# Setup of a two-layer transformer kernel: first loads in two parts, key splits and gates moved between engines

## What is computed

```python
ga = (2 * (ga >= 0) - 1) * maximum(abs(ga), 0.25)        # gb the same
# layer 0
h = layernorm(x) * (1 + ca) + sa
q, k, v = h @ Wq.T + bq, h @ Wk.T + bk, h @ Wv.T + bv    # 16 heads of 8
x = x + ga * (concat(softmax(q k^T / sqrt(8)) v) @ Wo.T + bo)
h = layernorm(x) * (1 + cb) + sb
x = x + gb * (shared_mlp(h) + top1_of_16_experts(h))
# layer 1: causal attention with 8 query heads over one shared key/value head of 16,
# then a gated feed-forward over each token and the one before it
```

## Time and profile before

| | |
|---|---|
| median of 3 runs | 1148.6 us (1145.84 to 1151.31) |
| profiled execution, its own time | 1150.95 us |
| its span | 1149.2 us |
| PE busy | 1027.6 us (89%) |
| DVE busy | 907.4 us (79%) |
| ACT busy | 819.5 us (71%) |
| POOL busy | 151.0 us (13%) |

### The profile page before, as it was taken

One profiled execution on the slowest core, in us unless ns is written; L12 is line 12 of the kernel. 1 busy time (PEld: TensorE's weight loads), 2 busy tenths in 40 slices (PEclk: granted clock), 3 DMA queues, 4 the chain that ended last, 5 costly groups with the idle time before them and its releaser, 6 DMA issues.

```text
span 1149.2 us, 22211 instructions
## 1 busy us (share of the span) xinstructions
PE 1027.6 (89%) x8772; PEld 351.4 (31%) x8772; DVE 907.4 (79%) x1174; ACT 819.5 (71%) x1581; POOL 151.0 (13%) x270
## 2 busy tenths in 40 slices
PE   4558999999999999999998999899978888798987
PEld 1212222222222222222232444343434453333314
DVE  5797999998999989999988777666766558587603
ACT  3105999998999998999986676467743546466775
POOL 2004100003000013000033000411031003000101
PEclk9757999999999999999999999999989999899987
DMA  4650500002000001000003331142003220200000
GB/s 106 122 103 15 139 2 2 2 2 43 2 2 2 2 15 29 2 1 3 2 1 111 113 100 29 29 89 52 2 1 111 67 63 22 46 10 2 10 2 10
DMA packets 47309, 42.07 MB, mean 37 GB/s; under 512 B 6150, under 2 KB 45414, under 8 KB 47206
## 3 DMA queue, kind: packets, MB, share of 16 engines
q1 hardware_dynamic: 44950, 35.27, 13.1%
q0 software_dynamic: 1824, 5.25, 1.6%
q10 hardware_dynamic: 432, 0.13, 0.0%
HBM read 26.83 MB, written 13.30 MB: 35 GB/s over the span
## 4 chain that ended last, share of the span: by engine, by line
PE 64%; DVE 18%; ACT 7%; DMA 4%; issue 3%; SPq 2%; POOL 1%; DVEq 0%; POOLq 0%; ACTq 0%
PE O L897 23%; PE T L868 12%; DVE mx L1204 10%; PE S L827 7%; PE S L834 4%; ACT PT L1435 3%; PE T L877 3%; PE S L1008 2%; PE S L966 1%; PE S L976 1%; PE T L1016 1%; DMA rows_k<-q 1%; PE S L967 1%; PE S L877 1%; PE T L906 1%
## 5 line engine op out<-in xcount | busy, mean ns | idle before, releaser
L1204 DVE TENSOR_REDUCE mx<-S 128x2 f32<-128x1024 f32 (+2 forms) x672 | 757.6, 1181 | 90.0 <-PE S L834 37.6
L1435 ACT ACTIVATE PT<-T 128x512 f32<-128x512 f32 (+2 forms) x1280 | 675.8, 580 | 118.4 <-PE T L868 47.8
L897 PE MATMUL O<-PT,Va 128*9 128x256 f32 (+1 forms) x4040 | 319.0, 388 | 3.3 <-ACT Os L1470 3.3
L827 PE MATMUL S<-Ks,Qs 48*128 48x512 bf16 x1024 | 208.2, 398 | 27.7 <-DVE mx L1204 20.9
L868 PE MATMUL T<-Qs,Ks 51*128 51x512 bf16 x1024 | 202.3, 388 | 16.0 <-ACT PT L1435 7.2
L868 PEld LDWEIGHTS T<-Qs,Ks 51*128 51x128 bf16 x1024 | 55.6, 93 | 227.1 <-issue 132.4
L897 PEld LDWEIGHTS O<-PT,Va 128*9 128x9 f32 x4040 | 60.0, 88 | 207.7 <-issue 198.3
L834 PE MATMUL S<-K,Qs 96*128 96x512 bf16 (+3 forms) x320 | 85.5, 357 | 15.0 <-DMA Qs<-rows_q 4.7
L877 PE MATMUL T<-Qs,K 99*128 99x512 bf16 (+3 forms) x256 | 72.2, 350 | 7.7 <-ACT PT L1435 4.1
L897 PE MATMUL O<-PT,V 128*17 128x512 f32 (+3 forms) x640 | 76.2, 549 | 0.0
L827 PEld LDWEIGHTS S<-Ks,Qs 48*128 48x128 bf16 x1024 | 52.6, 95 | 54.9 <-DVE mx L1204 47.0
(11 more groups left out here) (276 smaller groups left out, 836.1 us busy)
## 6 DMA issues: line engine op xcount, KB each, us to landing
Qs<-in_L_ffn_experts SPq DMA_DIRECT2D x28, 192.0 KB, 2.9
Ks<-in_L_ffn_experts SPq DMA_DIRECT2D x20, 192.0 KB, 2.6
Qs<-rows_q SPq DMA_DIRECT2D x48, 64.0 KB
Vf<-sorted_x SPq DMA_DIRECT2D x12, 256.0 KB, 4.7
sorted_y<-Vf SPq DMA_DIRECT2D x12, 256.0 KB, 2.3
Qs<-rows_q SPq DMA_DIRECT2D x24, 128.0 KB, 4.4
rows_q<-q SPq DMA_DIRECT2D x7, 384.0 KB, 2.6
sorted_x<-XP POOLq DMA_DIRECT2D x1, 1792.0 KB, 10.8
```

The lines of the kernel that those rows point to most:

```text
L827: m = e.matmul(two[:, i, :], Qs[r0:r0 + 48, hp, q0:q0 + 128], Ks[r0:r0 + 48, hp, CH * kb:CH * kb + CH], start=True, stop=True, tile_positi ...
L897: m = e.matmul(Ob[32 * g:32 * g + d1, lo:hi], v, PT[(2 * j + g // 2) % 4][:, p0 + lo:p0 + hi], start=(kt == 0 and halves[0] == 0), stop=Tr ...
L1204: e.tensor_reduce(mx[:, u % 2, h0:h0 + 2, kb], two[:, :, 0:n], AX.X, ALU.max).then_inc(free, 1)
L1435: e.activation(PT[(2 * j + pair) % 4][:, CH * i + lo:CH * i + CH], bank[:, lo:CH], ACT.Exp).then_inc(free, 1)
```

## The change

Setup order: statistics and norms of chunks 1 and 2 stand before the first splits; key chunks 1 to 3 are split by GpSimd, not VectorE; their projections use banks T2, O and T2. The loads of all four key chunks and of query chunk 0 are made in two parts: pair indices 0 and 1 first, and 2 to 7 in a second `load` that stands, with the late loads, after 16 score tiles. Of the first part of query chunk 0 SyncE issues six DMAs and ScalarE six. The four `values` stand after score tiles 8, 10, 12 and 14 instead of before the first. In the steps, `scaled_weights` moves from 1 to 5, `scaled_weights2` from 3 to 7, the projection of q chunk 1 from 5 to 9, `late_pool` from 8 to 11, `late_constants` from 12 to 14. `broadcast` and the arithmetic of `gates` go from VectorE to GpSimd; ScalarE copies the gates, `bias_v` and `rows` out of PSUM; GpSimd adds `bias_v` to the bias ahead of `scale`.

```diff
--- before.py
+++ after.py
@@ -21,6 +21,8 @@
 STORED = (16 * 7, 16 * 5)
 LOADED = {"k": 96, "q": 192, "k1": 48, "q1": 96}
 
+PARTS = {("k", c): 2 for c in range(4)} | {("q", 0): 2}
+
 
 GROUPS = ((0, 12, 0, 28), (12, 16, 28, 20))
 NT = 48
@@ -109,9 +111,18 @@
     P = Plan()
     loads = []
 
+    rest = []
+
     def load_slabs(keep=0):
         while len(loads) > keep:
-            P.stage("load", *loads.pop(0))
+            kind, c = loads.pop(0)
+            P.stage("load", kind, c, 0)
+            if (kind, c) in PARTS:
+                rest.append((kind, c))
+
+    def load_rest():
+        while rest:
+            P.stage("load", *rest.pop(0), 1)
 
     def project(kind, c, bank, over=()):
         P.project(kind, c, bank, over)
@@ -286,29 +297,29 @@
     P.stage("bias_q")
     P.stage("stats", 0, 1)
     project("q", 0, "S1a")
-    split("k", 0, "dv")
+    P.stage("stats", 0, 2)
     P.norm(0, 1)
     P.turn_h(0, 1, "T1")
+    P.stage("stats", 0, 3)
+    P.norm(0, 2)
+    split("k", 0, "dv")
     split("q", 0, "dv")
     load_slabs(1)
-    project("k", 1, "S1b")
-    P.stage("stats", 0, 2)
-    P.norm(0, 2)
-    load_slabs()
+    project("k", 1, "T2")
+    split("k", 1, "po")
     P.turn_h(0, 2, "T0")
-    split("k", 1, "dv")
-    project("k", 2, "S1a")
-    P.stage("stats", 0, 3)
     P.norm(0, 3)
     load_slabs()
+    project("k", 2, "O")
+    split("k", 2, "po")
     P.turn_h(0, 3, "T1")
-    split("k", 2, "dv")
-    project("k", 3, "S1b")
     load_slabs()
-    split("k", 3, "dv")
+    project("k", 3, "T2")
+    split("k", 3, "po")
     load_slabs()
     P.stage("constants")
-    for c in range(4):
+
+    def values(c):
         P.take(("v", c), ("O", "T2")[c % 2])
         P.stage("values", c)
 
@@ -326,11 +337,11 @@
     si = [0]
     now = [-2]
 
-    at(1, scaled_weights)
-    at(3, scaled_weights2)
-    at(5, lambda: project_q(1))
-    at(8, lambda: P.stage("late_pool"))
-    at(12, lambda: P.stage("late_constants"))
+    at(5, scaled_weights)
+    at(7, scaled_weights2)
+    at(9, lambda: project_q(1))
+    at(11, lambda: P.stage("late_pool"))
+    at(14, lambda: P.stage("late_constants"))
 
     def may_score():
         if si[0] >= len(tiles):
@@ -445,8 +456,13 @@
             k = max(k, -(-(due - si[0]) // (J2 - J + 1)))
         return min(k, MOST[L]) if may_score() else 0
 
-    for _ in range(many[0]):
+    for i in range(many[0]):
         emit_s()
+        if i in (7, 9, 11, 13):
+            values((i - 7) // 2)
+        elif i == 15:
+            load_rest()
+            P.stage("late_loads")
     for i in range(7):
         if i == 2:
             urgent.pop(0)[1]()
...
@@ -698,6 +714,14 @@
 
         def tile(v, j):
             return v[:, 128 * j:128 * j + 128]
+
+        def load_q(e, c, par, heads, loaded):
+
+            cols = slice(CH * c, CH * c + CH)
+            for j, part in enumerate((0, 0, 0, 1, 1, 2)):
+                r0 = 64 * par + 8 * j
+                src = scratch["q"][part, :, cols].rearrange("(d two h) n -> two d h n", two=2, h=8)[par]
+                e.dma_start(Qs[r0:r0 + 8, heads, cols], src[:, heads, :]).then_inc(loaded, 16)
 
         def late_loads():
             return ((woT[:, :], A["L0_attn_Wo"]),
@@ -819,16 +843,16 @@
                     two = Sb[turn[("s",) + tuple(a)][0]]
                     q0 = CH * c + 128 * qt
                     if L == 0:
-                        pe.wait_ge(rows_loaded["k", kb], LOADED["k"])
-                        pe.wait_ge(rows_loaded["q", c], LOADED["q"])
+                        pe.wait_ge(rows_loaded["k", kb, int(quad > 0)], LOADED["k"])
+                        pe.wait_ge(rows_loaded["q", c, int(quad > 0 and c == 0)], LOADED["q"])
                         hp = 2 * quad + pair
                         for i in range(2):
                             r0 = 64 * i
                             m = e.matmul(two[:, i, :], Qs[r0:r0 + 48, hp, q0:q0 + 128], Ks[r0:r0 + 48, hp, CH * kb:CH * kb + CH], start=True,
...
@@ -1079,30 +1103,6 @@
                 elif name == "bias_q":
                     dv.wait_ge(ld_w0, 64)
                     e.tensor_scalar(bqs[:, :], bq[:, :], 8.0 ** -0.5, None, ALU.mult).then_inc(bq_scaled, 1)
-                elif name == "broadcast":
-                    dv.wait_ge(silu_done, 1)
-                    dv.wait_ge(dv_const, 1)
-                    for l in range(2):
-                        m = e.tensor_scalar(cb[:, l, :], onesf[:, :], cs[:, l:l + 1], None, ALU.mult)
-                    m.then_inc(cb_made, 1)
-                    dv.wait_ge(ld_bv, 16)
-                    e.tensor_scalar(bvb[:, :], onesf[:, :], bv[:, 0:1], None, ALU.mult).then_inc(bv_made, 1)
-                elif name == "gates":
-                    bank, free = filled(("gates",))
-                    dv.tick(e.tensor_scalar(gt[:, 0:CH], bank[:, :], 0.0, 2.0, ALU.is_ge, ALU.mult))
-                    e.tensor_copy(gf, bank[:, :]).then_inc(free, 1)
-                    done(("gates",))
-                    dv.tick(e.scalar_tensor_tensor(gt[:, CH:], gf, -1.0, gf, ALU.mult, ALU.max))
-                    dv.settle()
-                    dv.tick(e.tensor_scalar(gt[:, CH:], gt[:, CH:], 0.25, None, ALU.max))
-                    dv.settle()
-                    dv.tick(e.scalar_tensor_tensor(gf, gt[:, 0:CH], -1.0, gt[:, CH:], ALU.add, ALU.mult))
-                    dv.settle()
-                    e.tensor_scalar(gH[:, :, :], gB[:, 1:4:2, :], 0.5, None, ALU.mult).then_inc(gates_made, 1)
-                elif name == "rows":
-                    bank, free = filled(("rows",))
...
@@ -1178,9 +1178,6 @@
                         e.scalar_tensor_tensor(v, tile(mt[:, 8, :], j), 1.0, bank[:, 0:128], ALU.add, ALU.mult).then_inc(free, 1)
                         done(("tail", part, j))
                         e.tensor_tensor(xs[:, t, :], xs[:, t, :], v, ALU.add).then_inc(mix_out, 1)
-                elif name == "bias_v":
-                    bank, free = filled(("bias_v",))
-                    e.tensor_tensor(boB[:, :], boB[:, :], bank[:, 0:128], ALU.add).then_inc(free, 1)
...
@@ -1404,13 +1401,26 @@
                         ac.wait_ge(ld_w0, 64)
                         e.activation(f, bank, ACT.Identity, bias=bk[:, :], scale=1.0).then_inc(free, 1)
                     else:
-                        e.activation(f, bank[0:rows], ACT.Copy, scale=1.0 if kind == "k1" else 128.0 ** -0.5).then_inc(free, 1)
+                        e.activation(f, bank[0:n_rows], ACT.Copy, scale=1.0 if kind == "k1" else 128.0 ** -0.5).then_inc(free, 1)
                     done((kind, c))
                     e.activation(parts[:, 0, :], f, ACT.Copy).then_inc(high_part, 1)
+                elif name == "load" and tuple(a) == ("q", 0, 0):
+                    ac.wait_ge(rows_stored[P.slot["q", 0]], 16)
+                    load_q(e, 0, 1, slice(0, 2), rows_loaded["q", 0, 0])
                 elif name == "values":
                     (c,) = a
                     bank, free = filled(("v", c))
                     e.activation(Va[:, four(c), :, 0:8], bank.rearrange("p (t h d) -> p t h d", t=4, h=16), ACT.Copy).then_inc(free, 1)
+                elif name == "gates":
+                    bank, free = filled(("gates",))
+                    e.activation(gf, bank, ACT.Copy).then_inc(free, 1)
+                elif name == "bias_v":
+                    bank, free = filled(("bias_v",))
+                    e.activation(bvb[:, :], bank[:, 0:128], ACT.Copy).then_inc(free, 1)
+                elif name == "rows":
+                    bank, free = filled(("rows",))
+                    e.activation(rows[:, 0, :], bank[:, 0:128], ACT.Copy)
+                    e.activation(rows[:, 1, :], bank[:, 128:256], ACT.Copy, bias=1.0).then_inc(free, 1)
                 elif name == "neg_turn":
                     L, u = a
                     bank, free = filled(("neg", L, u))
@@ -1619,10 +1629,35 @@
                                     channel_multiplier=-1).then_inc(po_const, 1)
                     for g in range(2):
                         e.dma_start(sorted_x3[g], XP[:, 0:1, :].to_broadcast([128, GROUPS[g][3], 128])).then_inc(zero_x, 16)
+                elif name == "broadcast":
+                    po.wait_ge(silu_done, 1)
+                    po.wait_ge(dv_const, 1)
+                    for l in range(2):
+                        m = e.tensor_scalar(cb[:, l, :], onesf[:, :], cs[:, l:l + 1], None, ALU.mult)
+                    m.then_inc(cb_made, 1)
+                    po.wait_ge(ld_bv, 16)
+                    e.tensor_scalar(bvb[:, :], onesf[:, :], bv[:, 0:1], None, ALU.mult).then_inc(bv_made, 1)
+                elif name == "gates":
+
+                    done(("gates",))
+                    sign, size = gt[:, 0:CH], gt[:, CH:]
+                    po.tick(e.tensor_scalar(sign, gf, 0.0, 2.0, ALU.is_ge, ALU.mult))
+                    po.settle()
+                    po.tick(e.tensor_scalar(sign, sign, -1.0, None, ALU.add))
+                    po.settle()
```

(29 more changed lines are left out.)

20 lines of the change are left out of this document (8 added, 12 removed).

## The result

The kernel after takes 1158.1 us in the median of four runs (1156.9 to 1161.7), the kernel before 1148.3 in the same series (1145.8 to 1151.3): a ratio of 1.0089, 95% interval 1.0055 to 1.0124. The change makes the kernel about 10 us **slower**; 1160 was forecast. The profiled execution took 1156.96 us (span 1155.2).

The account below looks back on a forecast made before the run. Settled stretches, with TensorE, VectorE and ScalarE full, stay untouched; what counts is when step 16 starts, set by waits up to 135.13 us. It comes 11.1 later: 1150.95 becomes 1162.0 profiled, 1160 as median, range 1144 to 1169.

Parts of the forecast that it names:

- The setup: Up to unit 0's end: first maximum about 29.3 instead of 37.20, unit 0 done near 69.8 instead of 74.94.
- the `values` stages: Four stages between score tiles of unit 0: each costs about 1.0 us (0 if fast), 4 us together.
- The start of the pass: Second pass (line 868), waiting for `nrow` behind SyncE's loads: starts at 80.5 us, 2.8 earlier; bounds 76.5 and 85.
- Steps 0 to 7: Second pass up to the gates: their products start 22.4 us after the pass, at 102.9, `mod` counted at 2.65.
- The gates on GpSimd: Gate arithmetic moved to GpSimd: 6.9 us, bounds 4.9 and 13.5, with each 512-column tensor_scalar taken at 1.16.
- The queue behind: GpSimd and SyncE after the gates: fills at 125.4, TensorE stopped some 11 us on `neg`, 20.9 from fills to `nrow` landing.
- Step 16: Start of unit 1's second pass, summing up everything earlier: at 146.2 us against 135.1, 11.1 later.
- The sum: Whole kernel: profiled 1150.95 us plus 11.1 gives 1162.0; the median, 2.35 lower, gives 1159.7, say 1160.
- equal units after that: Sign for the units after step 16: they take equal time in both kernels.
- Faster, GpSimd's work is hidden: Rival: step 16 waits for nothing, at 125.4 or 121.4; -9.7 to -13.7, 1135 to 1139 us; chance 0.14.
- No change, only GpSimd's order counts: Rival: fills and q1 loads do not crowd each other; step 16 at 138.0, +2.9, 1151.5 us; chance 0.17.
- Slower still: Rival: tensor_scalar at line 1680's price, gates 13.5 us instead of 6.9; +17.7, 1166 us; chance 0.12.

Follow-up runs that it names:

- e6: The kernel after with the 18 late loads moved behind the first `nrow` on SyncE: 1162.6 us, 1.0076 of the kernel before.
- the copies: The kernels before and after, both unchanged, run again side by side on one chip: 1154.8 and 1169.4 us, ratios 1.0005 and 1.0127.
- e7: The kernel after with the gates at step 14, q1 projection at 19, `late_pool` at 21, `late_constants` at 23: 1148.8 us, 0.9956 of the kernel before.
- e8: The kernel after with the changes of e6 and e7 together: 1144.5 us, 0.9906 of the kernel before.
- e5: The kernel after with only the two zero-fill DMAs moved from `late_pool` at step 11 to step 20: 1160.5 us, 1.0061 of the kernel before.

## Why the prediction was right, point by point

**The setup.** First maximum at 28.34 (29.3 forecast), unit 0 done at 66.46 (69.8). The term that was mis-sized is the `values` stages: 4 us forecast, 1.6 measured (the idle times 0.99 and 0.62 in the rows of the result; the other two cost nothing). I had said "each costs about 1.0 (0 if fast)": two ran slow (2.07 us each, at 35.81 and 38.79) and two at full speed (1.16, from 41.76).

**The start of the pass.** 79.23 against 80.5, for the reason given: SyncE is busy until `nrow` at 75.24. Most of the agreement is luck. The ones started at 37.50 (38.8) and held it 4.1 us, not 10.6, so SyncE was free 7.8 us sooner than forecast; but the second parts took 19.7 from then on (19 forecast), the late loads 13.8 (11), and `nrow` itself 4.0 from its first issue to the pass, where the sum has 1 although the same part quotes 4.0. e6 shows the reason directly. As a gain over the kernel before, 2.8 was forecast; it was 4.1 in the first pair of profiles and 2.1 in the copies.

**Steps 0 to 7.** From the pass to the gates' products 21.1 us (22.4 forecast). The difference is `mod`: it was carried over at 2.65 us from a stretch at the low clock, and stood behind the rise here. The chain of waits of the kernel after has

```profile
94.42 1.43 PE T L783 x12
```

**The gates on GpSimd.** 8.85 us against 6.9, inside the wide bounds (4.9 to 13.5) but just past the 8.5 that the forecast's own bounds used. The tensor_scalar of 512 columns, taken at 1.16, measured 1.94 with two operations and 1.50 or 1.51 with one; the products 1.27. The Trainium skill (GPSIMD Engine Reference, Engine selection) has one input near line rate, by which the gates would have taken 4.9 us by the prediction's estimate; the trace differs for this form, and it decides. The same section's factor of about 2 with two inputs agrees with 1.27 against VectorE's 0.69, a ratio of 1.8.

**The queue behind.** From the first scaling to the fills 13.09 us (13.1 forecast); fills at 124.63 (125.4). TensorE's stop on `neg`: from 117.9, 11.15 us long (from 118.6, some 11). From the fills to the landing 19.0 us where I carried over 20.86, since the q1 loads took 10.36 and not 12.60. Step 16 at 143.77 (146.2).

**The sum.** +8.5 at step 16 instead of +11.1, and +1.5 that I had not counted: the clock is low in the first half steps behind the stop (0.71 from 144 to 150 us). Errors of 1.3, 1.3 and 1.9 us one way and of 1.95 and 1.5 the other cancelled, so 1160 for 1158.1 is closer than its terms deserve. The step "equal units after that" held for layer 0 only: for the profiled execution the sum gave 1162.0 and 1156.96 was measured, since layer 1 gave back 4 us in that pair of profiles.

**The rivals.** "Faster, GpSimd's work is hidden" needed under 16 us of GpSimd work from the gates to `neg`; there were 25.7 (102.16 to 127.81). e7 and e8 show that it is true as soon as the same work stands behind `neg`. "No change, only GpSimd's order counts" fell with the 10.36 us of q1 loads; e5 shows that its condition (fills and loads apart: 4.14 us) gives step 16 at 136.06, where this rival had 138.0, and brings unit 2 back to 164.88. "Slower still" would have needed 3.2 us per tensor_scalar.

## What to carry to other kernels

A stage that is moved in one list moves in every engine's queue; before moving it, find in each in-order queue what stands behind it that another engine waits for, and count the unbroken work up to there. Idle time of an engine is cover only if it lies between the moved work and that item: GpSimd was idle for 25 us in the kernel before (32.56 in the kernel after), but before the gates. And put small transfers that someone waits for (`nrow`) ahead of large ones that nobody needs yet (late loads, zero fills): here the two together (e8), with no work removed, turned 0.9% slower into 0.9% faster.
